# Block sums on DVE and an undivided last half in a decoder layer

## The reference, cut to what matters

```python
kv = concatenate([context, latents], axis=1)          # 1601 + 256 = 1857 keys per batch
q = (latents @ Wq)  # 32 heads of 128                 # k, v: 8 heads of 128
q = rms_norm(q, q_norm_w); k = rms_norm(k, k_norm_w)
scores = einsum('bhgqd,bhkd->bhgqk', qg, k) / sqrt(128)
probs = softmax(scores, axis=-1)
out = einsum('bhgqk,bhkd->bhgqd', probs, v)           # 4 query heads share a key head
x = layernorm(x + out.reshape(...) @ Wo)
# router: w_sum and w_dense are the top 8 of softmax(x @ router_weight.T + router_bias)
x = layernorm(x + x * w_sum + w_dense @ expert_bias)
```

## Time and profile before

| | |
|---|---|
| median of three runs | 2812.35 us |
| the profiled execution | 2814.29 us |
| its span, first to last instruction | 2812.5 us |
| TensorE matmul busy | 2717.2 us, 97% |
| TensorE weight load | 2218.6 us, 79% |
| DVE | 2123.2 us, 75% |
| ScalarE | 2101.7 us, 75% |
| GpSimd | 2353.4 us, 84% |

### The profile page before, as it was taken

How to read it: one execution, slowest core, us unless ns; L and a number is a source line. 1 busy time by engine, 2 the same in 40 slices (tenths; PEclk the granted TensorE clock), 3 DMA queues, 4 the chain that set the end, 5 groups by cost and what they waited for, 6 DMA issues and landing times.

```text
span 2812.5 us, 48040 instructions
## 1 busy us (share of the span) xinstructions
PE 2717.2 (97%) x14812; PEld 2218.6 (79%) x14812; DVE 2123.2 (75%) x3532; ACT 2101.7 (75%) x4201; POOL 2353.4 (84%) x2320
## 2 busy tenths in 40 slices
PE   7899999999999999999999999999999999999975
PEld 5778778777878888888888888888888888888853
DVE  5577787877777877777777877777777878787873
ACT  3587777777777778777778887787787778777761
POOL 4299999898788888878889888888898888888893
PEclk9999999999999999999999999999999999999995
DMA  7656565565555454555545555554455445344310
GB/s 234 237 196 212 198 210 199 200 216 185 171 188 202 158 179 164 182 180 197 178 152 189 169 184 176 181 184 160 159 174 173 154 160 179 127 162 150 117 42 26
DMA packets 159435, 485.65 MB, mean 173 GB/s; under 512 B 16839, under 2 KB 27849, under 8 KB 159182
## 3 DMA queue, kind: packets, MB, share of 16 engines
q1 hardware_dynamic: 157592, 481.01, 50.9%
q10 hardware_dynamic: 1590, 1.58, 0.2%
HBM read 403.09 MB, written 79.43 MB: 172 GB/s over the span
## 4 chain that ended last, share of the span: by engine, by line
PE 82%; POOL 7%; issue 5%; DVE 3%; ACT 2%; DMA 1%; SPq 0%; ACTq 0%; POOLq 0%; DVEq 0%
PE K_ps L971 9%; PE K_ps L973 9%; PE K_ps L972 9%; PE OT_ps L1001 7%; PE S_ps L971 7%; PE S_ps L973 7%; PE S_ps L972 7%; PE OT_ps L971 5%; PE OT_ps L972 5%; PE OT_ps L973 5%; POOL acc L906 4%; PE F_ps L971 2%; PE F_ps L972 2%; PE F_ps L973 2%; POOL P_lo L888 2%
## 5 line engine op out<-in xcount | busy, mean ns | idle before, releaser
L906 POOL TENSOR_TENSOR acc<-acc,scores 128x512 f32<-128x512 f32 (+1 forms) x832 | 1105.3, 1328 | 53.0 <-ACT scores L1323 25.4
L888 POOL TENSOR_TENSOR P_lo<-scores,P_hi 128x512 fp32r<-128x512 f32 x672 | 891.8, 1327 | 215.4 <-ACT scores L1323 214.5
L1663 DVE SCALAR_TENSOR_TENSOR running_max<-S_ps,rk,running_max 128x512 f32<-128x512 f32 (+1 forms) x896 | 669.7, 747 | 304.7 <-ACT scores L1309 302.2
L1309 ACT ACTIVATE scores<-S_ps,rk 128x512 f32<-128x512 f32 (+1 forms) x960 | 652.5, 680 | 139.6 <-PE S_ps L973 121.3
L1647 DVE TENSOR_TENSOR scores<-scores,Mb_ps 128x512 f32<-128x512 f32 (+1 forms) x960 | 648.7, 676 | 135.5 <-PE Mb_ps L1127 135.4
L1322 ACT ACTIVATE P_hi<-scores 128x512 fp32r<-128x512 f32 x672 | 422.9, 629 | 265.3 <-DVE scores L1647 183.6
L1323 ACT ACTIVATE scores<-scores 128x512 f32<-128x512 f32 (+1 forms) x960 | 596.6, 622 | 15.2 <-DVE scores L1647 12.8
L971 PE MATMUL S_ps<-QT_hi,KT_hi 128*128 128x512 f32 (+1 forms) x960 | 496.2, 517 | 11.9 <-DVE running_max L1663 10.1
L971 PE MATMUL K_ps<-Wkv_hi,kvT 128*128 128x256 f32 (+1 forms) x1664 | 470.4, 283 | 2.4 <-DVE kvT L1713 2.4
L973 PE MATMUL K_ps<-Wkv_hi,kvT 128*128 128x256 f32 (+1 forms) x1664 | 470.7, 283 | 0.0
L972 PE MATMUL K_ps<-Wkv_lo,kvT 128*128 128x256 f32 (+1 forms) x1664 | 469.6, 282 | 0.0
(11 more groups left out here) (226 smaller groups left out, 4637.5 us busy)
## 6 DMA issues: line engine op xcount, KB each, us to landing
kvT<-kvT_scratch SPq DMA_DIRECT2D x403, 512.0 KB, 3.8
Wq_hi<-weight_halves_scratch SPq DMA_DIRECT2D x48, 512.0 KB, 5.3
Wq_lo<-weight_halves_scratch SPq DMA_DIRECT2D x48, 512.0 KB, 6.6
Wo_hi<-weight_halves_scratch SPq DMA_DIRECT2D x48, 512.0 KB, 4.7
Wo_lo<-weight_halves_scratch SPq DMA_DIRECT2D x48, 512.0 KB, 5.7
kvT_scratch<-built SPq DMA_DIRECT2D x45, 512.0 KB, 4.4
rinv_spread<-rinv_scratch SPq DMA_DIRECT2D x64, 256.0 KB, 4.9
Wkv_hi<-weight_halves_scratch SPq DMA_DIRECT2D x24, 512.0 KB, 5.6
```

The source lines that it names most:

```text
L888: e.tensor_tensor(P_lo[n % PB][0:r, :], prob(t)[0:r, :], f(P_hi[n % PB][0:r, :]), ALU.subtract)\
L906: e.tensor_tensor(a[0:r, :], a[0:r, :], prob(t)[0:r, :], ALU.add).then_inc(s_acc, 1)
L1309: e.activation(row[s % RING][0:r, :], S_ps[s % 2][0:r, :], ACT.Copy, scale=rk[0:r, v % 2, j:j + 1])\
L1663: e.scalar_tensor_tensor(a, src, k, a, ALU.mult, ALU.max).then_inc(s_top, 1)
```

## The change

In all halves but the last: the accumulator is no longer turned on TensorE. DVE reduces it with `apply_transpose` (`sum_blocks`): each 32x32 block is turned and summed, so that a [128, 512] tile gives [128, 16] with the partial sum of 32 keys of each query. TensorE adds the four groups of partitions with one product, whose moving operand `same` holds a one where partition and column agree modulo 32 (`add_blocks`). It comes out as 16x32, and DVE takes the reciprocal of that straight into `rrow`. RT is gone, and the division is placed six steps after AT.

In half 62 the tiles 2, 4, 6, 8, 10 and 12 are no longer added by GpSimd but summed by DVE one by one (`sum_tile`) into `sq`; in half 63 all fifteen are (`SUMMED`). The rows from 64 on of the last tile are zeroed for that by ScalarE before its 65 rows are copied in.

The last half (`LATE`) isn't divided. `OT_hi` and `OT_lo` are made from `OT_ps` directly, one head (256 columns) at a time, four jobs OL (`last_output`) project one head for one tile of queries, and DVE adds each to `y` scaled by the reciprocal of its rows, which is one number per partition there. The O jobs of halves 61 and 62 and their loads of Wo are put at earlier steps.

```diff
+    SUMMED = [[] for p in range(HALVES - 2)] + [[2, 4, 6, 8, 10, 12], list(range(NJ))]
+    ADDED = [NJ * p + j for p in range(HALVES) for j in range(1, NJ) if j not in SUMMED[p]]
+    LATE = [p for p in range(HALVES) if len(SUMMED[p]) == NJ]
...
-            12: [("RT", 2 * v - 3)],
...
-            27: [("RT", 2 * v - 2), ("QT", v, 1)],
+            27: [("QT", v, 1)],
...
+        if v == UNITS:
+            jobs = [x for x in jobs if x[0] != "O" or x[1] != HALVES - 3]
+            jobs += {19: [("O", HALVES - 3, 0)], 20: [("O", HALVES - 3, 1)]}.get(c, [])
+        if v == UNITS + 1:
...
+            jobs += {5: [("O", HALVES - 2, 0)], 6: [("O", HALVES - 2, 1)], 11: [("OL", 0, 0)], 12: [("OL", 1, 0)],
+                     13: [("OL", 0, 1)], 14: [("OL", 1, 1)]}.get(c, [])
...
-        return [x[1] for x in fill(s - 6) if x[0] == "RT"]
+        return [x[1] for x in fill(s - 6) if x[0] == "AT" and x[1] not in LATE]
...
-                 24: ("Wo", v - 1, 0)}.get(c)
+        chunk = {5: ("Wkv", v + 1, 0), 11: ("Wq", v + 1, 0), 13: ("Wq", v + 1, 1), (7 if v > UNITS else 14): ("Wo", v - 2, 1),
+                 (21 if v == UNITS else 24): ("Wo", v - 1, 0)}.get(c)
...
-                        e.wait_ge(s_ff, F_AT["AT", p - 2] + 1)
+                        e.wait_ge(s_bt, p - 1)
                     e.tensor_tensor(a[:], prob(t - 1)[:], prob(t)[:], ALU.add).then_inc(s_acc, 1)
...
-            def turn_sums(p):
-                e.wait_ge(s_acc, acc_no(NJ * p + NJ - 1))
+            def add_blocks(p):
...
+                e.wait_ge(s_bt, p + 1)
                 out = take(("AT", p))
-                for i in range(4):
-                    ins = e.transpose(out[:, i * P:(i + 1) * P], acc[p % 2][:, i * P:(i + 1) * P], ident[:])
...
+                e.matmul(out[0:16, 0:32], sums[:, p % 2, :], same[:, 0:32], start=True, stop=True).then_inc(s_ff, 1)
...
+            def last_output(t, g):
+                if t == 0:
+                    e.wait_ge(s_lh, g + 1)
+                if t == 0 and g == 0:
+                    e.wait_ge(s_wo, 32 * (2 * (UNITS - 1 - KVH) + 2))
+                out = take(("OL", t, g))
+                hi, lo = OT_hi[:, g, t * P:(t + 1) * P], OT_lo[:, g, t * P:(t + 1) * P]
+                e.matmul(out, hi, Wo_hi[:, g, :], start=True, stop=False)
+                e.matmul(out, hi, Wo_lo[:, g, :], start=False, stop=False)
+                if t == 0:
+                    e.wait_ge(s_ll, g + 1)
+                e.matmul(out, lo, Wo_hi[:, g, :], start=False, stop=True).then_inc(s_ff, 1)
...
+                    for g in range(2):
+                        e.activation(OT_hi[:, g, :], OT_ps[:, g * S:(g + 1) * S], ACT.Copy).then_inc(s_lh, 1)
...
+                elif job[0] == "OL":
+                    _, t, g = job
+                    e.wait_ge(s_pick, 2)
+                    e.scalar_tensor_tensor(y[:, t, :], out, last_rinv[:, 1, 2 * g + t:2 * g + t + 1], y[:, t, :],
+                                           ALU.mult, ALU.add).then_inc(s_fr, 1)
...
-                    e.reduce_sum(sums[:, p % 2, :], out.rearrange("p (i k) -> p i k", k=P), AX.X).then_inc(s_fr, 1)
-                    e.wait_ge(s_fr, F_AT[job] + 1)
-                    e.reciprocal(rinv[:, p % 2, :], sums[:, p % 2, :]).then_inc(s_ri, 1)
...
+                    e.reciprocal(rrow[:], out[0:16, 0:32]).then_inc(s_fr, 1)
...
+            def sum_tile(t):
+                p, j = divmod(t, NJ)
+                e.wait_ge(s_p, t + 1)
+                e.tensor_reduce(blocks_of(p)[:, SUMMED[p].index(j), :], prob(t).rearrange("p (j a) -> p j a", a=32), AX.X,
+                                ALU.add, apply_transpose=True).then_inc(s_bs, 1)
...
+            def sum_blocks(p):
...
+                added = acc[p % 2][:].rearrange("p (j a) -> p j a", a=32)
+                if not SUMMED[p]:
+                    e.wait_ge(s_acc, ADD_AT[NJ * p + NJ - 1] + 1)
+                    e.tensor_reduce(sums[:, p % 2, :], added, AX.X, ALU.add, apply_transpose=True).then_inc(s_bt, 1)
+                    return
...
+                if 0 <= s - WAIT - 1 < NS and summed_tile(s - WAIT - 1):
+                    sum_tile(s - WAIT - 1)
+                for x in fill(s + 1):
+                    if x[0] == "AT":
+                        sum_blocks(x[1])
```

More of the change, by code:

```diff
@@ L892, in add @@
                 p, j = divmod(t, NJ)
-                if j == 0:
+                if t not in ADD_AT:
                     return
@@ L1213, in _ @@
                     elif x[0] == "AT":
[L1214 removed]
+                        add_blocks(x[1])
                     elif x[0] == "FR":
```

130 lines of the change are left out of this document (97 added, 33 removed).

## The result

The changed kernel takes 2776.0 us (median of 4 runs, 2775.5 to 2776.8) against 2812.0 for the kernel before beside it. The ratio is 0.9871 (95% interval 0.9859 to 0.9884), so it is 36 us faster, where 53 were forecast. The account by landmarks explains the 38.8.

The account below looks back on a forecast made before the run. It took TensorE's stream to bound the kernel to 2660 us, GpSimd halves 62 and 63, then the last half's division and projection chain. Gains 24 + 5 + 12 + 12 = 53 us from 2812.35 gave 2759, range 2746 to 2776.

Parts of the forecast that it names:

- regime 1: Block sums, 200 to 2660 us: TensorE's instruction stream is the time; 0.42 us less a half over 59 halves, 24 us.
- The second rival: TensorE's saving in the block sums isn't time: 59 x 0.30 at half value, 9 us instead of 24, 2774; 12%.
- short waits will come up a little: Block sums: TensorE's waits for GpSimd and DVE grow slightly, so 24.8 us of saving become 24.
- Regime 2: The last two halves, at GpSimd's pace before: tile sums on DVE save 5 us in half 62 and 12 in half 63.
- the 29 taken: Half 62: DVE's 27.8 us of work come to about 29 with its waits, so DVE ends the half.
- the 25.7: Half 63: time from its first shift to the last P V product, 37.7 us before, so 12 us less.
- the loop over P_hi: Half 63: cycling through three P_hi buffers takes 1.2 to 1.35 us a tile, nearly the same pace as DVE's sum.
- Regime 3: The last half's division and projection after its last product: 18.9 us become 7, with Wo arriving late, 12 us less.
- the two rivals on it: DVE's turned reduction takes two passes, 1.3 us, 2773, 13%; or four passes, 2.7 us, slower than before, 2842, 3%.
- OT_n of half 62: In the last half: taken near its median of 0.95 us; as a rival, blocked for 5.92, 6 us back, 2765; 10%.
- The clock: Rival: denser work in the last half keeps the clock at 2.4 GHz into the router, 5 us, 2754; 10%.

Follow-up runs that it names:

- e2: The changed kernel with a second fp32 product of 128x16 by 128x32, on constants, for each of halves 0 to 62: 2801.0 us.
- e3: The changed kernel with OT_n, OT_hi and OT_lo of halves 0 to 60 made two steps later, where they stood before the change: 2768.3 us.
- e10: e3 with the one fp32 product of halves 0 to 60 placed two steps later and everything else where it was: 2767.7 us.
- e5: The changed kernel with each of the 21 tile sums of the last two halves made twice, first into a spare tile: 2788.0 us.
- e4: The changed kernel with the block product of the even halves put behind the four fp32 transposes of K instead of ahead: 2777.9 us.
- e12: e10 with split totals and two single-pass products in the odd halves 3 to 49 alone: 2767.0 us.
- e8: e3 with the additions of tiles 1, 4, 7 and 10 of the last half back on GpSimd and the accumulator reduced there: 2770.4 us.

## Why the prediction was off, and where it held

The forecast was 2759 with a range up to 2776, and the kernel took 2776.0, at the very end of it. Direction and regimes were right; the size of one term was not.

- **The step that failed: regime 1, 24 us, came to 9.8.** Three things lie in it.
  - *The price of the product.* The prediction said: "The new one has half the moving columns and an eighth of the weight columns, so each instruction may cost half, 0.12 in all." It costs 0.36 (e2). It isn't proportional to its size: the router's 16 instructions in 1.90 us stand in one run of their own kind, while a lone small product also holds up what is ahead of it. Net 0.20 a half instead of 0.42; for the 60 halves whose product stands ahead of half 62, 12 us instead of 25. The second rival's numbers came, 9 us for regime 1 and 2774, but not its mechanism: it took 0.30 a half and made half of that time, and the record has 0.20 a half, all of it time. That the two agree is luck.
  - *The division.* The change list has it ("the division is placed six steps after AT"), and as AT is two steps ahead of RT, it moved by two steps. The prediction costed every operation but not this move. OT_n, which has two inputs in SBUF, fell right behind QT_lo in the odd halves, and beside a GpSimd that splits weights it took up to 2.76 us there. That took 8 us back (e3), 1.7 of it by the clock in half 5.
  - *A gain that wasn't forecast.* With e10, which has neither the early division nor a dearer product, the first scores of half 62 are 17.7 us earlier than before, 5.7 more than 60 x 0.20. They come in four halves, 14, 52, 56 and 60 (1.0, 1.1, 1.1 and 2.6 us beyond the usual step). In the halves 52, 56 and 60 TensorE waited 1.76 us for the running maximum before and 0.77 after, and in half 60 the rest is the stretch at the lower clock that is gone. The prediction took the clock of regime 1 as 1.00 throughout, and its "short waits will come up a little" had the sign wrong in these halves. What shortened the wait stays open. At its step DVE lost the reduction of 0.68 and a reciprocal, ahead of the router's selection of the top experts, but it has the turned reduction a few steps earlier in the same half. Behind the selection a two-input operation on 128x128 took 1.10 us before and 0.44 after. Whether it is DVE's smaller load at that step or the moment at which it meets GpSimd was not taken apart by a run.
  - Together: 12 + 6 - 8 = 10.
- **Regime 2.** Half 62: 3.5 for 5. DVE ends it, as argued, and e5 shows it; its waits were 1.4 us more than the 29 taken. Half 63: 26.04 for the 25.7. In five other kernels with the same work in it (e2, e3, e4, e10, e12) that half takes 25.56 to 26.03, so the 0.3 says nothing. Of the two reasons given for the number, e5 bears out DVE's sum in part; the loop over P_hi stays argued. GpSimd's 33.87 us for 26 operations make 1.30 each and not 1.28, which changes neither term.
- **Regime 3.** 13.5 for 12. The order of arrival was right, Wo comes last, but the projection starts 0.9 us behind the last P V product (TensorE idle for 0.6 of it) and not 1.6 to 2: the load was issued from 2738.19 on, 4.2 us ahead of that end, and not 3.3.
- **DVE's turned reduction** took 0.70 for the 0.68, so the two rivals on it fell. Its wait for GpSimd's last addition was 0.8 us in two places, rightly costed at nothing.
- **OT_n of half 62** was not blocked (0.65), as forecast; with four more additions on GpSimd it was, for 3.28 (e8). **The clock** was 0.93 in half 63 and 1.00 in the last projection, where it had been 0.69 to 0.71 before, but 0.54 in the router again: its 16 logit instructions take 3.68 us as in the earlier trace rows, so that rival fell, except that the twelve products of the projection ran at the full clock.
- **The prediction's own range** doesn't follow from its ends: 15 to 29 in regime 1 and 5 either way in the tail make 2749 to 2773, not 2748 to 2771.
- The test named in the prediction, a pair of halves shorter by 0.84 us, was the right one: it read 0.40, and TensorE full beside it told that the stream was longer than thought, not that it wasn't the bound.

The version to keep is e3 or e10, 2768.3 and 2767.7 us, 8 us under the change and 45 under the kernel before; e12 is no different by what the runs can tell.

## What to carry to other kernels

Price a lone small matmul by the starts around it, not by a share of a long run of its kind; where no trace has one, put a spare one in and measure, which is what told here. When a step is taken out, look at what was placed relative to it: the order of DVE changes, and an operation with two SBUF inputs can take four times its own time at another place. On DVE beside a busy GpSimd, count the operations with two SBUF inputs and the casts from SBUF to SBUF, not their elements. Before a wait of TensorE is priced, look at the granted clock behind it.
